# Local attention of a Perceiver stack: features and values as three bf16 products of high and low parts

## The reference, cut to what matters

```
q  = h @ q_w.T + q_b
k  = h @ k_w.T + k_b
v  = h @ v_w.T + v_b
ph = _phrase_states(h)            # running mean inside chunks of 32 tokens
pk = ph @ pk_w.T + pk_b
pv = ph @ pv_w.T + pv_b
...
top_sc, top_l = jax.lax.top_k(scores, TOPK)
...
all_sc = jnp.concatenate([seq_score[..., None], top_sc, phr_score[..., None]], axis=-1)
all_v = jnp.concatenate([v_prev[:, :, None, :], sem_v, pv_prev[:, :, None, :]], axis=2)
w = jax.nn.softmax(all_sc, axis=-1)
out = jnp.einsum('bsn,bsnd->bsd', w, all_v)
```

## Time and profile before

| | us |
|---|---|
| median of 3 runs | 2565.54 (2564.16 to 2569.23) |
| span of the profiled execution | 2560.5 |
| the local attention stage in it, barrier to barrier | about 101 (2395.6 to 2496.6) |
| TensorE busy in the span | 2287.2 |

### The profile page before, as it was taken

The page is one execution under the profiler, slowest core; times in us unless marked ns, Lnnn a source line. Parts: engine busy times, 40 slices in busy tenths (PEclk is TensorE's granted clock), DMA queues, the critical chain, the costliest instruction groups (busy, mean ns, idle before and its releaser), DMA issues. The chain is left out here.

```text
span 2560.5 us, 57277 instructions
## 1 busy us (share of the span) xinstructions
PE 2287.2 (89%) x21679; PEld 1495.6 (58%) x21955; DVE 1822.7 (71%) x3379; ACT 1569.7 (61%) x2922; POOL 1126.8 (44%) x894
## 2 busy tenths in 40 slices
PE   4499999999999999998888799995789899998795
PEld 2245665666566655665546477773467677676442
DVE  4467877888788877777354599995777777766236
ACT  3346666666666666665335299893477777787313
POOL 2345676666766675555200000002467676656100
PEclk9699999999999999998999799997999999998897
DMA  4322243224322331123421499994443434224002
GB/s 150 97 69 79 74 120 86 75 76 120 92 74 76 86 89 42 40 63 98 171 91 56 171 343 364 365 329 167 154 128 121 128 120 131 87 90 163 29 1 84
DMA packets 256131, 313.63 MB, mean 122 GB/s; under 512 B 71521, under 2 KB 182881, under 8 KB 254961
## 3 DMA queue, kind: packets, MB, share of 16 engines
q1 hardware_dynamic: 251904, 301.82, 36.6%
q10 hardware_dynamic: 3312, 6.03, 0.6%
q0 software_dynamic: 640, 2.10, 0.3%
HBM read 226.30 MB, written 47.91 MB: 107 GB/s over the span
## 5 line engine op out<-in xcount | busy, mean ns | idle before, releaser
L678 POOL TENSOR_TENSOR a_plo<-a_p,a_phi 128x512 bf16<-128x512 f32 x272 | 316.3, 1163 | 357.6 <-ACT a_phi L734 356.8
L940 PE MATMUL ps<-w,a_xhi 128*128 128x512 bf16 x1086 | 412.7, 380 | 6.3
L941 PE MATMUL ps<-w,a_xhi 128*128 128x512 bf16 x1086 | 412.8, 380 | 0.3 <-issue 0.2
L942 PE MATMUL ps<-w,a_xlo 128*128 128x512 bf16 x1071 | 407.1, 380 | 0.1
L2101 POOL TENSOR_TENSOR a_plo<-a_p,a_phi 128x512 bf16<-128x512 f32 x256 | 307.3, 1201 | 173.6 <-ACT a_phi L2138 164.6
L700 ACT ACTIVATE a_kraw<-ps 128x256 f32<-128x256 f32 x272 | 104.5, 384 | 357.0 <-PE ps L942 355.7
L2233 DVE CUSTOM_DVE_ANT_0 a_junk<-ps,a_biasrow 128x512 bf16<-128x512 f32 x256 | 176.2, 688 | 110.1 <-PE ps L2373 86.4
L757 DVE TENSOR_TENSOR a_v<-ps,a_v 128x256 bf16<-128x256 f32 x272 | 114.4, 420 | 161.7 <-ACT a_v L702 160.4
L2133 ACT ACTIVATE a_p<-ps,a_mcol 128x512 f32<-128x512 f32 x256 | 175.0, 684 | 82.8 <-PE ps L2391 75.2
L771 DVE SCALAR_TENSOR_TENSOR a_kraw<-a_kraw,a_rn 128x1024 f32<-128x1024 f32 (+1 forms) x80 | 155.2, 1940 | 77.5 <-POOL a_rn L637 77.5
L637 POOL TENSOR_TENSOR a_rn<-a_rn,a_power 128x16 f32<-128x16 f32 (+1 forms) x80 | 204.2, 2552 | 6.7
(11 more groups left out here) (452 smaller groups left out, 6783.6 us busy)
## 6 DMA issues: line engine op xcount, KB each, us to landing
e_wst<-in_L_ffn_W SPq DMA_DIRECT2D x46, 2048.0 KB, 10.9
a_ks<-a_khi SPq DMA_DIRECT2D x256, 64.0 KB, 2.0
a_ks<-a_klo SPq DMA_DIRECT2D x256, 64.0 KB, 2.0
a_ct<-in_ctxT SPq DMA_DIRECT2D x16, 1024.0 KB, 6.7
a_ks<-k1h_d SPq DMA_DIRECT2D x128, 128.0 KB, 2.5
xa<-in_ctx SPq DMA_DIRECT2D x8, 1024.0 KB, 5.9
a_xn<-in_ctx SPq DMA_DIRECT2D x8, 1024.0 KB, 5.5
k1h_d<-a_khi SPq DMA_DIRECT2D x64, 128.0 KB, 2.0
```

The source lines that it names most:

```text
L678: pool.tensor_tensor(p_lo[:, m % 3, :], p32[:, m % 2, :], p_hi[:, m % 3, :], ALU.subtract)\
L940: pe.matmul(out, x_hi[:, c, tile], w_hi[:, c, g, :], start=(c == 0), stop=False)
L941: pe.matmul(out, x_hi[:, c, tile], w_lo[:, c, g, :], start=False, stop=False)
L942: last = pe.matmul(out, x_lo[:, c, tile], w_hi[:, c, g, :], start=False, stop=(c == C - 1))
```

## The change

Both factors of the features and of the values are split into a bf16 high part and a bf16 low part, and each f32 product becomes three bf16 products that add up in the same bank: high by high, high by low, low by high. The parts are made in the stage:

- weights: ScalarE copies `w[k]` to bf16 (`w_hi`, 128x2048 in one instruction), GpSimd subtracts (`w_lo`). ScalarE makes the first high part ahead of the norm's square root, the second behind the copies of the turned tokens, and the others between the copies of the features (ahead of groups 4, 6 and 8);
- turned tokens: ScalarE's copies out of PSUM write bf16 (`ht_hi`) in place of the f32 `l_ht`, VectorE subtracts from the same bank (`ht_lo`) ahead of the scaling of the running sums;
- running means: ScalarE copies `PT_` to bf16 (`pt_hi`) in the first four steps of its feature loop, GpSimd subtracts (`pt_lo`).

The transposes, the prefix products, the scores and all that follows stay in f32.

```diff
+            def weights_low(k):
+                pool.wait_ge(w_hi_done, k + 1)
+                pool.tensor_tensor(w_lo[:, k], w[k], w_hi[:, k], ALU.subtract).then_inc(w_lo_done, 1)
+
+            weights_low(0)
+            weights_low(1)
+            for c in range(C):
+                pool.wait_ge(pt_hi_done, c + 1)
+                pool.tensor_tensor(pt_lo[:, c, :], PT_[:, c, :], pt_hi[:, c, :], ALU.subtract).then_inc(pt_lo_done, 1)
+            for k in range(2, 5):
+                weights_low(k)
...
+            def weights_high(k):
+                act.wait_ge(w_in[k], 16)
+                act.activation(w_hi[:, k], w[k], ACT.Copy).then_inc(w_hi_done, 1)
+
+            weights_high(0)
             norm.scalar(act)
-            turn.scalar(act, ps, HT)
+            for c in range(C):
+                act.wait_ge(h_turn, c + 1)
+                act.activation(ht_hi[:, c, :], ps[:, c, :], ACT.Copy).then_inc(ht_hi_done, 1)
+            weights_high(1)
             act.wait_ge(c_in, 7 * 16)
             for n in range(3 * C):
+                if n < C:
+                    act.wait_ge(pf_cp, n + 1)
+                    act.activation(pt_hi[:, n, :], PT_[:, n, :], ACT.Copy).then_inc(pt_hi_done, 1)
+                elif n % 2 == 0 and n < C + 6:
+                    weights_high(2 + (n - C) // 2)
                 act.wait_ge(f_mm, n + 1)
...
             norm.vector(dve, step, Hn, X)
+            for c in range(C):
+                dve.wait_ge(ht_hi_done, c + 1)
+                dve.tensor_tensor(ht_lo[:, c, :], ps[:, c, :], ht_hi[:, c, :], ALU.subtract).then_inc(ht_lo_done, 1)
...
-            pe.wait_ge(turn.copied, C)
+            pe.wait_ge(ht_lo_done, C)
             for n in range(3 * C):
                 k, o = n // C, n % C
                 if o == 0:
-                    pe.wait_ge(w_in[k], 16)
+                    pe.wait_ge(w_lo_done, k + 1)
                 if n == 2 * C:
-                    pe.wait_ge(pf_cp, C)
+                    pe.wait_ge(pt_lo_done, C)
...
                 for c in range(C):
-                    last = pe.matmul(ps[:, 4 + n % 2, :], w[k][:, c, o * P:(o + 1) * P],
-                                     (HT if k < 2 else PT_)[:, c, :], start=(c == 0), stop=(c == C - 1))
+                    pe.matmul(out, w_hi[:, k, c, cols], hi[:, c, :], start=(c == 0), stop=False)
+                    pe.matmul(out, w_hi[:, k, c, cols], lo[:, c, :], start=False, stop=False)
+                    last = pe.matmul(out, w_lo[:, k, c, cols], hi[:, c, :], start=False, stop=(c == C - 1))
...
                 if b == 0:
-                    pe.wait_ge(w_in[3 + k], 16)
+                    pe.wait_ge(w_lo_done, 4 + k)
...
                 for c in range(C):
-                    last = pe.matmul(ps[:, bank_v(n), :], (HT, PT_)[k][:, c, b * P:(b + 1) * P], w[3 + k][:, c, :],
-                                     start=(c == 0), stop=(c == C - 1))
+                    pe.matmul(out, hi[:, c, tok], w_hi[:, 3 + k, c, :], start=(c == 0), stop=False)
+                    pe.matmul(out, hi[:, c, tok], w_lo[:, 3 + k, c, :], start=False, stop=False)
+                    last = pe.matmul(out, lo[:, c, tok], w_hi[:, 3 + k, c, :], start=False, stop=(c == C - 1))
```

More of the change, by code:

```diff
@@ L2483, in local1 @@
     Hn = sb("l_h", [P, B, D], F32)
-    HT = sb("l_ht", [P, C, TOK], F32)
+    ht_hi = sb("l_hthi", [P, C, TOK], BF16)
+    ht_lo = sb("l_htlo", [P, C, TOK], BF16)
     PT_ = sb("l_pht", [P, C, TOK], F32)
+    pt_hi = sb("l_pthi", [P, C, TOK], BF16)
+    pt_lo = sb("l_ptlo", [P, C, TOK], BF16)
+    w_hi = sb("l_whi", [P, 5, C, D], BF16)
+    w_lo = sb("l_wlo", [P, 5, C, D], BF16)
     w4 = sb("l_w4", [P, C, D], F32)
-    w = [keep["lw"][:, k] for k in range(4)] + [w4]
+    w = [keep["lw"][:, k] for k in range(4)] + [w4[:]]
     bc = sb("l_bc", [P, 3, C], F32)
@@ L2507, in local1 @@
     norm = Norm(sb, sem, "ln")
-    turn = Turn(sem, "lt", C, [0, 1, 2, 3])
+    h_turn, ht_hi_done, ht_lo_done = sem("l_hturn"), sem("l_hthi_d"), sem("l_htlo_d")
+    pt_hi_done, pt_lo_done = sem("l_pthi_d"), sem("l_ptlo_d")
+    w_hi_done, w_lo_done = sem("l_whi_d"), sem("l_wlo_d")
     w_in = keep["lw_in"] + [sem("l_w_in4")]
@@ L2529, in _ @@
             sp.dma_start(w4[:], t["l_pvT"].rearrange("(c p) n -> p c n", p=P)).then_inc(w_in[4], 16)
+        @block.gpsimd
+        def _(pool):
+            def weights_low(k):
[8 more added lines that the diff above has]
+                weights_low(k)
         @block.scalar
         def _(act):
+            def weights_high(k):
+                act.wait_ge(w_in[k], 16)
+                act.activation(w_hi[:, k], w[k], ACT.Copy).then_inc(w_hi_done, 1)
+            weights_high(0)
             norm.scalar(act)
-            turn.scalar(act, ps, HT)
+            for c in range(C):
+                act.wait_ge(h_turn, c + 1)
+                act.activation(ht_hi[:, c, :], ps[:, c, :], ACT.Copy).then_inc(ht_hi_done, 1)
+            weights_high(1)
             act.wait_ge(c_in, 7 * 16)
             for n in range(3 * C):
+                if n < C:
[3 more added lines that the diff above has]
+                    weights_high(2 + (n - C) // 2)
                 act.wait_ge(f_mm, n + 1)
@@ L2611, in _ @@
             pe.wait_ge(norm.done, B)
-            turn.tensor(pe, ps, Hn, identf)
+            for c in range(C):
+                for b in range(B):
+                    last = pe.transpose(ps[:, c, b * P:(b + 1) * P], Hn[:, b, c * P:(c + 1) * P], identf[:])
+                last.then_inc(h_turn, 1)
             pe.wait_ge(c_in, 7 * 16)
@@ L2624, in _ @@
                 if o == 0:
-                    pe.wait_ge(w_in[k], 16)
+                    pe.wait_ge(w_lo_done, k + 1)
                 if n == 2 * C:
-                    pe.wait_ge(pf_cp, C)
+                    pe.wait_ge(pt_lo_done, C)
                 if n >= 2:
                     pe.wait_ge(f_cp, n - 1)
+                hi, lo = (ht_hi, ht_lo) if k < 2 else (pt_hi, pt_lo)
+                out, cols = ps[:, 4 + n % 2, :], slice(o * P, (o + 1) * P)
                 for c in range(C):
-                    last = pe.matmul(ps[:, 4 + n % 2, :], w[k][:, c, o * P:(o + 1) * P],
-                                     (HT if k < 2 else PT_)[:, c, :], start=(c == 0), stop=(c == C - 1))
+                    pe.matmul(out, w_hi[:, k, c, cols], hi[:, c, :], start=(c == 0), stop=False)
+                    pe.matmul(out, w_hi[:, k, c, cols], lo[:, c, :], start=False, stop=False)
+                    last = pe.matmul(out, w_lo[:, k, c, cols], hi[:, c, :], start=False, stop=(c == C - 1))
                 last.then_inc(f_mm, 1)
@@ L2644, in _ @@
                 if b == 0:
-                    pe.wait_ge(w_in[3 + k], 16)
+                    pe.wait_ge(w_lo_done, 4 + k)
                 if n >= 6:
                     pe.wait_ge(v_cp, n - 5)
+                hi, lo = ((ht_hi, ht_lo), (pt_hi, pt_lo))[k]
+                out, tok = ps[:, bank_v(n), :], slice(b * P, (b + 1) * P)
                 for c in range(C):
-                    last = pe.matmul(ps[:, bank_v(n), :], (HT, PT_)[k][:, c, b * P:(b + 1) * P], w[3 + k][:, c, :],
-                                     start=(c == 0), stop=(c == C - 1))
+                    pe.matmul(out, hi[:, c, tok], w_hi[:, 3 + k, c, :], start=(c == 0), stop=False)
+                    pe.matmul(out, hi[:, c, tok], w_lo[:, 3 + k, c, :], start=False, stop=False)
+                    last = pe.matmul(out, lo[:, c, tok], w_hi[:, 3 + k, c, :], start=False, stop=(c == C - 1))
                 last.then_inc(v_mm, 1)
```

## The result

The changed kernel has a median of 2551.19 us (2542.43 to 2557.17), the kernel before, on the same chip, 2564.16 us. The ratio is 0.9943, with an interval from 0.9929 to 0.9958, which is 11 to 18 us; the forecast was 13.8 us and 2551.7.

The account below looks back on a forecast made before the run. TensorE's almost unbroken chain bounds the local attention stage after 5.6 us of norm set by VectorE. Products -16.8, norm +2.95, turned tokens +0.05 give -13.8 us: span 2546.7 plus 5.0 is 2551.7 us, range 2548.6 to 2554.6.

Parts of the forecast that it names:

- The products: Features and values on TensorE: 20 groups of three bf16 products per f32 product fall from 68.7 to 51.9 us, -16.8 us.
- The parts arrive in time: Features and values: all splitting hidden by TensorE at no cost, third weight early by 3.4 us; rival that splits bind 7%.
- the copy of feature 4: ScalarE's copy out of feature 4, claimed delayed to T0 + 13.3 to 14.0 by the third weight's high part, but hidden.
- T0: The start of the features on TensorE, from which the arrival times of the split parts are counted.
- VectorE's chain beside the values: Top-k and softmax weights: some 5 us of VectorE work follow the fourth value group against 10.4 us of TensorE, which ends last.
- The turned tokens: Copies to bf16 and VectorE's four subtractions ahead of the running sums' scaling: features start 0 to 0.1 us later, 0.05 taken.
- The norm: Start of the stage: GpSimd's first subtraction holds VectorE's L86, +2.95 us; forecast with a hold 80%, no hold 9%.
- the bound of 2.45 us: Norm: the cost if the tiny L86 passes and only the L90 are held; time 2551.2, counted with the forecast.
- a shared bandwidth: Norm: VectorE and GpSimd merely share bandwidth, the four L90 cost some 2 us in all, time 2550.8 at most.
- A second pair: VectorE's `l_neg` beside a later GpSimd subtraction: may be held too, at no cost, since nobody waits for it before the scores.
- The whole: Sum of products, norm and turned tokens: -16.8 + 2.95 + 0.05 = -13.8 us, for a time of 2551.7 us.
- The 5 us between span and time: Whole kernel: the runs' median 2565.5 us lies 5.0 us above the profiled span, a difference claimed to carry over.

Follow-up runs that it names:

- e2: Changed kernel with the low by low product added to each group of features and values, four bf16 products: median 2571.06 us, ratio 1.0017 to the kernel before.
- e3: Changed kernel with one of the three bf16 products left out of every group, all splitting kept: stage 71.9 us, run once.
- e1: Changed kernel with one added wait, so GpSimd's first subtraction starts after the norm: median 2553.92 us, ratio 0.9955 to the kernel before, stage 83.8 us.
- e6: Changed kernel with GpSimd's first subtraction after the norm and q-k scores waiting only for their own eight features: 2552.64 us, ratio 0.9952, stage 82.75 us.
- e7: The changed kernel unedited, run again in later side by side rounds: median 2553.01 us, ratio 0.995 to the kernel before.
- e4: Changed kernel with the first weight's low part made in four GpSimd subtractions of 128x512 in place of one of 128x2048: stage 86.2 us, run once.
- e5: Changed kernel with the first two weights split at the start of the stage, two GpSimd subtractions behind one another: stage 90.7 us, run once.
- e0: The changed kernel unedited, run again for comparison: median 2555.26 us against 2568.07 before, ratio 0.995, stage 86.8 us.

## Why the prediction was right

**The products: right.** Forecast -16.8 us. Measured -10.12 for the features with their gap and -6.75 for the values, -16.87. e2 showed that the number of bf16 products is the reason.

**The parts arrive in time: right.** No gap in the features, the third weight's low part early by 3.5 us (forecast 3.4). ScalarE's and GpSimd's rows of the change at this place:

```profile
2420.50 1.90 ACT L2556 ACTIVATE l_whi<-c_hi 128x2048 bf16<-128x2048 f32 x1
2422.50 0.69 ACT L2572 ACTIVATE l_qkp<-ps,l_bc 128x512 f32<-128x512 f32 x1
```

```profile
2422.48 4.07 POOL L2542 TENSOR_TENSOR l_wlo<-c_hi,l_whi 128x2048 bf16<-128x2048 f32 x1 [2.72 <-ACT l_whi L2556]
```

One reading of the prediction was wrong without harm: it called the copy of feature 4 delayed, to T0 + 13.3 or later. By its own terms this copy can't start sooner than T0 + 5 x 2.60 + 0.27 = T0 + 13.3, since group 4 has to end first. It started at T0 + 13.15, exactly 2.59 us behind that of feature 3, so the high part ahead of it delayed nothing. The working put the third weight's parts 0.2 us too late (T0 + 17.4 against T0 + 17.20 for the low part), and so did that of e3 (T0 + 14.0 against T0 + 13.74), which is why the gap at feature 8 that it named didn't come. The 0.9 us at features 6, 8 and 10 do not follow from its terms at all: a copy of feature 4 that starts at T0 + 9.8 ends at T0 + 10.5, 0.1 us behind the time at which feature 6 wants the bank (T0 + 10.4). In e3 the right place to look was VectorE's chain beside the values, for which the prediction had room and the expectation of e3 did not work out a number.

**The turned tokens: a small term that is not constant.** The copies to bf16 took 0.60 us, as in f32, and the four `l_htlo` 0.69 us each. In the first profile of the change TensorE never waited for them. But the scaling of the running sums stands behind them in VectorE's list, and where TensorE's clock rose early, TensorE waited for it inside the prefix products: 0.22 us in e1 and e6, and in e7, the change itself:

```profile
2412.72 2.05 PE L2658 MATMUL ps<-l_prefix,l_h 128*128 128x128 f32 x16 [0.36 <-DVE l_pht L2592]
```

So the term, 0 to 0.1 us in the forecast, runs from 0 to 0.36.

**The norm: right.** Forecast 3.1 us for L86 and 2.95 us for the start of TensorE; measured 3.13 and 8.50 - 5.54 = 2.96. The row that carried this was a single one of another stage, a 128x4 tensor_scalar of 3.94 us, of the same form as L86. Without it, L86 and its four elements would have looked too small to be held, and the bound of 2.45 us (only L90 held) would have been the natural choice. The alternative that the prediction weighed against the Trainium skill, a shared bandwidth, is refuted by e4 and e5. The Trainium skill, SBUF — State Buffer, section "Who interferes with whom", also states that an instruction of VectorE with at most one SBUF input and outside the two-port modes is not concerned. The aggregate L84 (0.38 us inside the subtraction) and the reciprocal in e5 (0.18 us) agree. A second pair in the change bears the hold out, which the prediction named as possible and of no cost. These are GpSimd's second subtraction and VectorE's `l_neg`, a tensor_scalar that took 0.22 us before:

```profile
2407.46 4.07 POOL L2542 TENSOR_TENSOR l_wlo<-c_hi,l_whi 128x2048 bf16<-128x2048 f32 x1 [8.66 <-ACT l_whi L2556]
```

```profile
2410.16 1.45 DVE L2595 TENSOR_SCALAR l_neg<-l_lower 128x128 f32<-128x128 f32 x1
```

It ends at 2411.61, 0.08 us behind the subtraction, while the last two scalings of the running sums, with one input in PSUM, took their 0.69 us each inside the same subtraction.

**Not in the sum: +0.47 and -0.24 us.** The transposes and prefix products took 8.07 us against 7.60, and the end of the stage, from L2655 to the next bn_stats, 10.76 against 11.00. The first is the clock. Windows of 1 us from the start of the transposes show it at 0.50 (1.2 GHz) for four of them before, then 0.93, and for five after, then 0.94. This was not the longer idle time ahead: in e0 and e2, with the same 10.6 us of idle time, the two steps took 7.58 and 7.67 us. So the moment at which the clock rises varies from one execution to the next, and with it the length of the two steps, by about 0.9 us over the kernels here (7.3 us in e7, of which 0.36 are a wait, to 8.2 in e3 and e5). The second is the barrier: VectorE's idle time ahead of the next stage was 1.37 us in before and 1.12 in all profiles of the changed kernel and its edits. Why stays open.

**The whole.** 13.8 forecast, 13.7 in the stage. That the medians agree to half a microsecond is luck, since the median of the same kernel was 2551.2, 2555.3 and 2553.0 in three comparisons, and that of before 2564.2, 2568.1 and 2566.2. The ratios, 0.9943, 0.995 and 0.995, are what repeats. The 5 us between span and time, which the prediction carried over, are no constant either: the profiled execution of the change took 2546.12 us, 1.9 above its own span. The forecast doesn't hang on them, since 2565.5 - 13.8 gives the same 2551.7.

## What to carry to other kernels

Splitting an f32 product in three bf16 products saves a quarter of the product's time where TensorE is the unbroken chain (3.43 us a group became 2.59), and no more; the cost lies in where the splitting falls. A GpSimd subtraction with its operands in SBUF held a VectorE tensor_scalar that started beside it until its own end, however small the latter was (four elements: 3.13 us in place of 0.17), so keep long GpSimd subtractions off short chains of VectorE on which everybody waits: here one added wait took the 3 us off the stage and opened no gap beyond 0.22 us. In a program whose other stages scatter by several microseconds, measure the stage, barrier to barrier, not the span.

## What the runs showed of the hardware that was not expected

Four bf16 products of 128x512 with four weight loads took the same time as one f32 product, as e2 expected, within 0.6% (42.38 against 42.14 us for 12 groups with their gap). Four subtractions of 128x512 on GpSimd in place of one of 128x2048 let VectorE's instructions in between them, and the two engines took turns: the four L90 took 3.90 us, against 1.92 us alone and 5.15 us in e5, where a whole 128x2048 was in the way. TensorE's clock rose 2.7 us (e7) to 5.5 us (e3) after the same work began, though the idle time ahead of it was 10.6 us in both. And the gap ahead of the scores, 0.78 us of idle time in the row, cost 1.05 us: that is what its removal gave in e6.
